# Attention on one Trainium2 core: the turned probabilities leave PSUM through two engines instead of one

## What is computed

```python
q = (x @ Wq) / sqrt(32);  k = x @ Wk;  v = x @ Wv;  bias = x @ Wb
gate = sigmoid(x @ Wg + bg)
attn = softmax(einsum('ijhd,ikhd->ijkh', q, k) + bias, axis=k)
out  = gate * einsum('ijkh,ikhd->ijhd', attn, v)
x    = x + out @ Wo + bo
```

## Time and profile before

| | |
|---|---|
| median of 3 runs | 1241.21 us (1240.4 to 1241.44) |
| the profiled execution | 1242.17 us, its span in the trace 1240.40 us |
| busy share of the span | TensorE 89%, its weight loads 62%, VectorE 59%, ScalarE 46%, GpSimd 26% |
| attention loop | from 160.3 us to about 459 us of the span |
| in 300 to 350 us | TensorE 47.1 us busy, VectorE 39.7, ScalarE 34.7, GpSimd 29.9; granted TensorE clock 1.00 |

### The profile page before, as it was taken

One profiled execution on the slowest core, in us unless ns is written; L12 is line 12 of the kernel. 1 busy time (PEld: TensorE's weight loads), 2 busy tenths in 40 slices (PEclk: granted clock), 3 DMA queues, 4 the chain that ended last, 5 costly groups with the idle time before them and its releaser, 6 DMA issues. The chain is left out here.

```text
span 1240.4 us, 25484 instructions
## 1 busy us (share of the span) xinstructions
PE 1098.8 (89%) x9447; PEld 770.5 (62%) x9447; DVE 728.6 (59%) x3560; ACT 569.3 (46%) x1161; POOL 325.6 (26%) x466
## 2 busy tenths in 40 slices
PE   3677289999999969994999999999999999999688
PEld 2422067777777743443777677677777767776476
DVE  2521057787877752224566766766676677667235
ACT  1299556767676631002444444444444444443200
POOL 0100046656565631000112212221221122122111
PEclk9987679999999988995999999999999999999869
DMA  8000000000000000000000000000000000000002
GB/s 156 1 0 4 4 4 3 2 3 2 3 2 3 3 1 1 1 0 9 2 1 1 1 2 1 1 2 1 1 2 1 1 1 1 1 1 1 1 29 112
DMA packets 11487, 11.35 MB, mean 9 GB/s; under 512 B 4324, under 2 KB 9188, under 8 KB 11364
## 3 DMA queue, kind: packets, MB, share of 16 engines
q1 hardware_dynamic: 9266, 9.08, 2.9%
q10 hardware_dynamic: 2098, 0.65, 0.3%
HBM read 5.14 MB, written 4.23 MB: 8 GB/s over the span
## 5 line engine op out<-in xcount | busy, mean ns | idle before, releaser
L1460 PE MATMUL quad<-theta,nat 128*128 128x512 f32 x512 | 240.7, 593 | 0.0
L639 POOL TENSOR_TENSOR nat<-nat,arena 128x512 f32<-128x512 f32 x128 | 132.9, 1050 | 111.4 <-DVE arena L703 111.4
L1259 POOL TENSOR_TENSOR nat<-nat,const 128x512 f32<-128x512 f32 x32 | 40.6, 1268 | 439.4 <-DVE nat L1398 439.4
L1468 PEld LDWEIGHTS quad<-flat 128*128 128x128 f32 x768 | 104.6, 190 | 46.5 <-ACT flat L1290 25.1
L1468 PE MATMUL quad<-flat 128*128 128x128 f32 x768 | 123.8, 284 | 2.8 <-ACT flat L1290 1.7
L1460 PEld LDWEIGHTS quad<-theta,nat 128*128 128x128 f32 x512 | 87.5, 191 | 61.7 <-issue 61.7
L703 DVE CUSTOM_DVE_ANT_0 nat<-quad,arena 128x128 f32<-128x128 f32 x512 | 113.2, 283 | 9.7 <-PE quad L789 9.7
L1290 ACT ACTIVATE flat<-quad 128x256 f32<-128x256 f32 x192 | 73.4, 382 | 70.4 <-PE quad L1468 56.6
L662 ACT ACTIVATE nat<-bank 128x512 f32<-128x512 f32 x128 | 69.5, 595 | 57.2 <-PE bank L797 57.2
L1367 DVE SCALAR_TENSOR_TENSOR flat<-nat,c,duo 128x128 f32<-128x128 f32 x64 | 22.0, 345 | 102.0 <-PE duo L1477 102.0
L667 ACT ACTIVATE nat<-nat 128x512 f32<-128x512 f32 x128 | 77.2, 633 | 5.6 <-POOL nat L639 5.5
(11 more groups left out here) (384 smaller groups left out, 2316.2 us busy)
## 6 DMA issues: line engine op xcount, KB each, us to landing
out<-nat SPq DMA_DIRECT2D x16, 256.0 KB, 2.0
arena<-flat SPq DMA_DIRECT2D x64, 4.0 KB
const<-in_constants ACTq DMA_DIRECT2D x1, 400.5 KB, 3.2
arena<-in_L_conv_Ws SPq DMA_DIRECT2D x1, 240.0 KB
flat<-arena SPq DMA_DIRECT2D x3, 32.0 KB, 4.3
nat<-in_x SPq DMA_DIRECT2D x4, 0.2 KB, 13.0
arena<-in_L_conv_Wq ACTq DMA_DIRECT2D x1, 32.0 KB, 7.8
arena<-in_L_conv_Wk ACTq DMA_DIRECT2D x1, 32.0 KB, 7.7
```

The costliest lines, as they stand in the source:

```text
L639: pool.tensor_tensor(scored, scored, of_head(least[b], h).broadcast_to([128, ROWS, L]), ALU.subtract).then_inc(lowered, 1)
L1259: pool.tensor_tensor(quarters(rem), quarters(rem), ident.unsqueeze(1).broadcast_to([128, ROWS, 128]), ALU.add).then_inc(diag_added, 1)
L1460: return pe.matmul(m.quad[:, n, :], vT[:, col(n)], m.theta[:, part, :], start=(part == 0), stop=False, skip_group_check=True)
L1468: last = pe.matmul(m.quad[:, row, place * C:(place + 2) * C], a8[g % 2][:, col(row)], zs[half][k % 2][:, n, :], start=False, stop=(k == 2) ...
```

## The change

The copies of rows 0 and 2 (bank 0, `turn_a`) stay on ScalarE; those of rows 1 and 3 (bank 1, `turn_b`) go to VectorE, as a `tensor_copy` of the same shape. VectorE does the first between the reciprocal and head 1's reductions, the second between heads 1 and 2. They signal a semaphore of their own, `odd_kept`; `kept` now counts two a group. TensorE's order is the same: row 3's turn waits for `odd_kept`, and L779 and L803 wait for both. The signal that the output weights are halved now goes to `wo_ready`, on top of the DMA's 16.

```diff
--- before.py
+++ after.py
@@ -589,7 +589,7 @@
     qk_made, q_ready, k_ready = S("qk_made"), S("q_ready"), S("k_ready")
     gv_made, v_ready, th_ready = S("gv_made"), S("v_ready"), S("th_ready")
     scores_made, shifted, lowered, exps_done = S("scores_made"), S("shifted"), S("lowered"), S("exps_done")
-    turned, kept = S("turned"), S("kept")
+    turned, kept, odd_kept = S("turned"), S("kept"), S("odd_kept")
     av_made, sums_made, sums_kept, sums_turned = S("av_made"), S("sums_made"), S("sums_kept"), S("sums_turned")
     rtotal_ready, rwide_ready, r_made, factor_ready, gated_ready = S("rtotal_ready"), S("rwide_ready"), S("r_made"), S("factor_ready"), S("gated_ready")
     out_made, x1_ready, swapped = S("out_made"), S("x1_ready"), S("swapped")
@@ -659,7 +659,7 @@
                 act.wait_ge(turned, 4 * g + r + 1)
                 if r == 0 and g > 0:
                     act.wait_ge(sums_made, g)
-                act.activation(pT[r], m.bank[r % 2][:, :], ACT.Copy).then_inc(kept, 1)
+                act.activation(pT[r], turn_a[:, :], ACT.Copy).then_inc(kept, 1)
 
             def exponentials(g, b, h):
                 act.wait_ge(lowered, HEADS * g + h + 1)
@@ -677,7 +677,7 @@
             for g in range(GROUPS + 1):
                 own, past = g < GROUPS, g >= 1
                 if past:
-                    for r in range(ROWS):
+                    for r in range(0, ROWS, 2):
                         keep_turn(g - 1, r)
                 if own:
                     exponentials(g, g % 2, 0)
@@ -704,8 +704,12 @@
                                                     -1.0, BIG, ALU.add, ALU.min, least[b][:, at(r, h, 1)])
                 last.then_inc(shifted, 1)
 
+            def keep_odd_turn(g, r):
+                dve.wait_ge(turned, 4 * g + r + 1)
+                dve.tensor_copy(pT[r], turn_b[:, :]).then_inc(odd_kept, 1)
+
             dve.wait_ge(wo_ready, 16)
-            dve.tensor_scalar(wo, wo, 0.5, None, ALU.mult).then_inc(S("wo_halved"), 1)
+            dve.tensor_scalar(wo, wo, 0.5, None, ALU.mult).then_inc(wo_ready, 1)
             dve.wait_ge(m.sem("bias_laid"), 16 * 64)
             for g in range(STEPS0):
                 b = g % 2
@@ -721,8 +725,13 @@
                         dve.wait_ge(rwide_ready, g - 2)
                     dve.reciprocal(rtotal.rearrange("p (r h) -> p r h", r=ROWS),
                                    total_bank[:, 0:128].rearrange("p (r x) -> p r x", r=ROWS)[:, :, 0:HEADS]).then_inc(rtotal_ready, 1)
+                if past:
+                    keep_odd_turn(g - 1, 1)
                 if own:
                     shift_head(g, b, 1)
+                if past:
+                    keep_odd_turn(g - 1, 3)
+                if own:
                     shift_head(g, b, 2)
                 if older:
                     dve.wait_ge(r_made, g - 1)
@@ -814,7 +823,7 @@
 
             pe.wait_ge(pick_ready, 1)
             project_qk(0)
-            pe.wait_ge(S("wo_halved"), 1)
+            pe.wait_ge(wo_ready, 16 + 1)
             for g in range(STEPS0):
                 b = g % 2
                 own, past, older = g < GROUPS, 1 <= g <= GROUPS, g >= 2
@@ -831,9 +840,10 @@
                     pe.wait_ge(v_ready, g)
                     turn(g - 1, 0)
                     turn(g - 1, 1)
-                    for r in range(2, ROWS):
-                        pe.wait_ge(kept, 4 * (g - 1) + r - 1)
-                        turn(g - 1, r)
+                    pe.wait_ge(kept, 2 * (g - 1) + 1)
+                    turn(g - 1, 2)
+                    pe.wait_ge(odd_kept, 2 * (g - 1) + 1)
+                    turn(g - 1, 3)
                 if older:
                     pe.wait_ge(rwide_ready, g - 1)
                     for r in range(ROWS):
@@ -844,7 +854,8 @@
                     project_qk(g + 1)
                 if own:
                     if past:
-                        pe.wait_ge(kept, 4 * g)
+                        pe.wait_ge(kept, 2 * g)
+                        pe.wait_ge(odd_kept, 2 * g)
                     project_gv(g)
                 if older:
                     pe.wait_ge(gated_ready, g - 1)
```

## The result

The changed kernel is slower by half a percent: 1247.50 us median of 5 runs (1245.29 to 1248.46) against 1241.21 us of before, ratio 1.0045 with a 95% interval of 1.003 to 1.0059. The forecast was 1249.6, in a range of 1245.0 to 1255.5. The execution whose profile follows is the one with 1245.29 us; its span is 1243.5. So the two spans differ by 3.1 us only. From the first scores to the last factor the changed kernel's trace is 6.2 us longer (301.4 against 295.2); the part ahead of that is 1.1 us shorter and the part behind it 2.0 us shorter, though nothing differs there but the signal for the output weights.

The account below looks back on a forecast made before the run. TensorE was taken to set the attention stage's pace. Added steps and edges, 7.25 + 0.61 + 0.32 + 0.19 = 8.4 us on the 1241.21 us median, gave 1249.6 us, range 1245.0 to 1255.5.

Parts of the forecast that it names:

- The path: Attention step: VectorE's copies delay factor and gated product, so TensorE's output projection starts later, 0.25 us per step.
- The cost of a copy: Each 128x512 float32 copy from PSUM on VectorE lasts about 692 ns but takes a queue slot of 0.61 us.
- Rival 2: VectorE copies cost all of their length or more, by a drained queue or shared PSUM reading: 1252 to 1256; chance 0.13.
- rival 1: VectorE copies hide in the old wait plus slack if each slot is under 0.49 us: 1241.2 us; chance 0.08.
- The slack: Before TensorE's output projection: it could have started 0.36 us earlier, so that much lateness of VectorE's product is free.
- The size: Attention step grows by 0.25 us on TensorE's path, from 8.97 to 9.22 us.
- The factor's lateness: VectorE's factor (L732): 1.32 us added ahead, 0.71 of them into the old wait, so 0.61 us later.
- The edges: Attention stage's first and last steps: g = 31 adds 0.61 us, g = 1 adds 0.32, g = 32 adds 0.19.
- What was to be hidden: Fourth turn's slip of 0.07 us, even 0.1, vanishes behind TensorE's wait for L645; the 0.25 us wait for ScalarE's copy remains.
- Rival 3: Faster: emptier queues bring GpSimd's L645 earlier, removing TensorE's 0.28 us wait in 27 steps; 1234 at best; chance 0.04.
- Rival 4: The clock: more TensorE idle drops its granted clock to 0.50; two such steps cost 13 us, beyond 1262; chance 0.03.
- The sign that the prediction named for the new wait: TensorE waits before the output projection for VectorE's gating product, some 29 more steps, about 0.2 us of profiled idle time.

Follow-up runs that it names:

- Run 5: Changed kernel with GpSimd's widening (L645) ahead of head 0's subtraction (L639) instead of behind it: step 9.16 us, 1247.62 us, ratio 1.0061 to the kernel before.
- run 7: Changed kernel with head 2's reductions behind the factor and gated product on VectorE, head 3's behind the residual: step 8.97 us, 1242.97 us, ratio 1.0017.
- run 3: Changed kernel with both VectorE copies taking only 256 of 512 columns, the rest left out: step 8.97 us, 1240.35 us, ratio 0.9985 to the kernel before.
- the five points above: Scores-to-factor distance and step (us) of the changed kernel (5.23, 9.16) and four variants of its copies: 4.67, 8.97; 4.87, 8.97; 5.18, 9.12; 5.80, 9.73.
- run 6: Kernel before the change, with GpSimd's widening (L645) ahead of head 0's subtraction (L639): step 8.47 us, 1227.00 us, ratio 0.9887.
- run 2: Changed kernel with only row 3's copy on VectorE, rows 0 to 2 copied by ScalarE: step 9.12 us, 1245.84 us, ratio 1.0034 to the kernel before.

## Why the prediction held, step by step

- **The path.** Predicted: scores, head 0, copy, head 1, copy, head 2, factor, product, output projection. The trace has this chain without a gap on VectorE from 304.87 to the end of L747, and its pieces make up the step: 5.23 us from the scores to the factor, 0.72 to the gated product, 0.74 to the output projection and 2.47 to the next scores, together 9.16. Run 5 shows that the wait for GpSimd adds nothing to it, and run 7 that the step falls to 8.97 when the factor comes earlier with the same copies.
- **The cost of a copy.** 691 ns in the median and a slot of 0.61 and 0.60 us, as taken from L327 and from L738's successor. Rival 2, the full duration, is out, and so is rival 1. Of the two rules that rival 1 took from the Trainium skill's page "VectorE: DVE Perf Modes", the copies agree with "Why PSUM operands drop a tier": 256 columns take 0.42 us (run 3) and 512 take 0.69, so about 1.05 ns for each further column. The single rate, one column in a cycle of the page's 0.96 GHz, is 1.04 ns.
- **The slack.** 0.36 predicted, 0.37 by the five points above.
- **The size.** 0.25 us a step predicted, 0.19 measured. The factor's lateness was the mis-sized term: 0.56 us (5.23 - 4.67) instead of 0.61, against a slack of 0.37 instead of 0.36. The first copy started 0.25 behind the reciprocal and not 0.27, the second copy's slot was 0.60, and each head's reductions took 0.84 and not 0.85. A few hundredths each, but only what exceeds the slack counts, so a tenth too much lateness became a third too much cost; times 29 steps that is 1.7 us, most of the 2.1 us between 1249.6 and 1247.5. The five executions themselves spread over 3.2 us, so that the medians agree this closely with the sums is partly luck; the steps, which differ by a few hundredths at most, are the better test.
- **The edges.** In the trace the steps g = 31 and 32 grew by 0.56 (7.51 to 8.07) and 0.20 (7.49 to 7.69); predicted 0.61 and 0.19. In g = 1 the wait for head 1 is there (0.18 us ahead of L782), but from first reduction to first reduction the step grew by 0.09 only, not 0.32; TensorE stood at a higher clock there than before (the first two turns took 1.09 us against 1.29). These 0.20 us would bring the 0.09 to 0.29, near the 0.32, but no run shows why the clock rose earlier in this execution. The first 29 full steps together went from 260.1 to 265.7 us. 5.6 + 0.56 + 0.20 + 0.09 = 6.4 us; the medians differ by 6.3.
- **What was to be hidden.** The fourth turn did slip by 0.05 us (1.19 instead of 1.14) and TensorE's wait for L645 shrank by as much (0.23 instead of 0.28). The wait for ScalarE's copy stayed at 0.25, and ScalarE has 64 copies left. Rival 3 had the wait for L645 as its place; it is indeed the place where 14 us lay (run 6), but the change did not touch it. Rival 4 did not occur: the granted clock was 1.00 from 180 to 440 us in both. The sign that the prediction named for the new wait, about 0.2 us of idle time ahead of the output projection, came as 0.31 us in the row of the weight loads, below the 0.35 that would have spoken for rival 2, and not at all in the row of the matmuls.

## What to carry to other kernels

Before work is moved to an engine that looks idle, find the consumer that waits for that engine behind the new place, and count lateness there. What counted here was how late the factor and the product came: VectorE's old idle time ahead of the factor plus the slack of the output projection were free, all beyond them counted in full. Where in the queue the work goes can matter more than how much it is: with head 2 moved behind the gated product and head 3 behind the residual two copies cost nothing in a step (run 7), while in the old order one copy alone cost 0.15 us (run 2). And an engine's short wait in every step is worth a look for a change of order at the releasing engine: exchanging two instructions of GpSimd gained 14 us (run 6), while no split of the copies tried here gained anything.

## What the runs showed of the hardware that I had not expected

The idle time that the profile puts ahead of a TensorE instruction can understate what the wait costs. The wait for L645 was shown as 0.28 us, and taking it away shortened the step by 0.50. The rows show where the rest was: before, L840 started 306.05 - 304.62 = 1.43 us behind the third turn; in run 6 it starts 0.99 behind it, 0.44 us less, and the projection follows after 0.53 us and not 0.58. The profile counts idle time only from the modelled end of the matmul before. Without the wait L840 starts at 307.70, 0.15 us ahead of the end of the turns at 306.71 + 1.14 = 307.85; these 0.15 and the 0.28 shown make up the 0.44 to within a hundredth.

```profile
306.71 1.14 PE L797 MATMUL bank<-const,nat 128*128 128x128 f32 x8 [0.25 <-ACT nat L662]
307.70 0.60 PE L840 MATMUL duo<-const,arena 128*128 128x128 f32 x4
308.23 1.13 PE L773 MATMUL quad<-flat,w 64*128 64x256 f32 x8
```

In the changed kernel the new wait does not show in the matmuls' rows either. It costs 0.19 us a step: from the projection L791 to the output projection L863 it is 310.32 - 309.59 = 0.73 us, and between the same two before 308.57 - 308.03 = 0.54 (the row below). It stands only in the row of the weight loads, as 0.31.

```profile
308.03 0.61 PE L782 MATMUL bank<-w,flat 64*128 64x128 f32 x8
```
